# The order in which an instruction's semaphore waits are listed, for exponentials, turns, products and value products

## The chip, the cores and the metric

The kernel runs on one core of one Trainium2 chip. The metric is the device time in microseconds (us) of one execution, as the median of several runs. Besides the timed runs there is one execution taken by the hardware profiler; all durations below come from that one.

## What is computed

A small tower over 16 sequences of 512 tokens with 64 channels, in float32: token features, attention with 8 heads over one shared key and value, and a mixture of six experts of which two are taken per token. Cut to what matters here:

```python
h = tok(x, hour, month, day)                       # sines, two layers, layer norm, residual
n = layernorm(h)
q = einsum('bsc,oc->bso', n, Wq)                   # 8 heads of 64
k = einsum('bsc,oc->bos', n, Wk); v = n @ Wv       # one key and one value for all heads
attn = softmax(q k / sqrt(8))
h = h + (attn v, heads side by side) @ Wo
e = layernorm(h)
h = h + sum over the top two of six experts of weight * expert(e)
```

## The kernel before

The 16 sequences are worked in 8 pairs. The instructions of all five engines are written out by hand in one program; semaphores alone order the engines. A pair has 64 slots (`SLOTS`), and each step has the slot at which its engine issues it (the tables `A`, `P`, `F`, `Z`, `L` at the head of the file). In the slots of pair i the attention of pair i runs, beside the preparation of pair i+1 (`prep`) and the experts of pair i-1 (`ffn`).

- TensorE, `scores` (line 427; matmuls at 438): every second slot it writes two banks of scores of 128 x 512. `queries` (443, 450) makes the folded queries, `pv` (454, 470) multiplies the exponentials with the output weights scaled by one over the softmax sum, in two parts of 16 matmuls, for 64 groups of heads in all. `value_products` (553, 560) multiplies the turned result with the values. `turn_halves` (480), `values` (491), `tokens` (507, 518, 533), the router (602, 613) and the experts (627, 638, 662) fill the rest.
- VectorE: `maxima` (865, 868) takes minus the row maximum of each 128 x 512 scores and tells `maxed`; `recip_sums` (871, 874) inverts the sums and tells `rzd`; `turn` (876, 880) transposes the result of `pv` out of its bank and tells `mtd`.
- ScalarE: `exps` (736, 742) takes the exponential of a score bank into one of three kept buffers `p` and tells `expd`, 512 times; `queries_out` (748), `values_out` (758) and expert activations (796) copy other banks out.
- GpSimd (POOL): `over_sums` (289, 295) scales the output weights by the inverse sums and tells `wozd`.

All products land in four double banks (`s_bank`), which a planner (`ring_places`) hands out in the order of the program. Before a bank is written, `free` (387) waits for the step that read it last: `expd`, `mtd`, `gsb`, `e1_sb` and so on. The helper `wait` (280) skips waits for values of zero or less; its `wait_ge` is line 284. `pvd` tells that a `pv` is done, `fin_ps` that the value products of a pair are, `v_sb` that values were copied, `hatt_sb`, `y_ps`, `y_pool` belong to the experts' side.

An instruction can have several waits: the calls of `wait_ge` that stand between it and the instruction before it. The change touches nothing but their order.

Of the kernel before, what the change touches and what calls it, by code (L numbers as in the profile page):

```python
# [17 lines left out]
HH = HP // 2  # L18
# [26 lines left out]
KEPT = 3  # L45
# [136 lines left out]
def tower(nc, ids, consts, out):  # L182
# [4 lines left out]
    with ctx:  # L187
# [11 lines left out]
        def k(name):  # L199
            return cst[:, LAYOUT[name][0]:LAYOUT[name][1]]  # L200
# [48 lines left out]
        def bank(*what):  # L249
            return ring[place[what][0]]  # L250
# [29 lines left out]
        def wait(eng, s, value):  # L280

            if value <= 0:
                return
            eng.wait_ge(s, value)
# [95 lines left out]
        def _(pe):  # L380
            def half(r):
                return slice(64 * r, 64 * r + 64)

            def quarter(r):
                return slice(32 * r, 32 * r + 32)
# [68 lines left out]
            def pv(i, a, part):  # L454

                kept = (HH * i + a) % KEPT
                if part == 0:
                    free("PV", i, a)  # L460
                else:
                    pe.wait_ge(pv_half, HH * i + a + 1)
                for mm in range(4):
                    if not part and mm % 2 == 0:
                        pe.wait_ge(wozd, 2 * (HH * i + a) + mm // 2 + 1)
                    for r in range(2):
                        hh = (r + part) % 2
                        keys = p[half(r), 8 * kept + 2 * mm + hh, :].rearrange("q (n h o) -> q h n o", n=8, h=2)
                        for q in range(2):
                            last = pe.matmul(bank("PV", i, a)[half(q), 512 * hh:512 * hh + 256], woz[half(r), kept, 2 * mm + hh, :],  # L470
                                             keys[:, q, :, :], start=(part == 0 and mm == 0), stop=(part == 1 and mm == 3),
                                             skip_group_check=True)
                last.then_inc(pvd if part else pv_half, 1)
# [79 lines left out]
            def value_products(i, par, *heads):  # L553


                for n in range(8):
                    for g4 in range(4):
                        q, s2 = g4 // 2, g4 % 2
                        for b2, first, end in heads:
                            last = pe.matmul(  # L560
                                bank("FIN", i, s2)[half(b2), 512 * q + 32 * first:512 * q + 32 * end],
                                v[quarter(g4), par, b2, n, :], m[quarter(g4), b2, first:end, n, :],
                                start=(n == 0), stop=(n == 7), skip_group_check=True)
                return last

            def fin_part(n):

                i, par = PAIRS - 1, (PAIRS - 1) % 2
                if n == 0:
                    pe.wait_ge(v_sb, 2 * i + 2)  # L570
                pe.wait_ge(mtd, HH * i + HH - 2 + n)
                if n == 0:
                    free("FIN", i, 0)
                    free("FIN", i, 1)
                value_products(i, par, *(((0, 0, 8), (1, 0, 4)), ((1, 4, 6),), ((1, 6, 8),))[n]).then_inc(fin_parts, 1)

            def ffn(i, par, slot, f=F):

                if f is not L and slot == f["FIN"]:
                    pe.wait_ge(v_sb, 2 * i + 2)  # L580
                    pe.wait_ge(mtd, HH * i + HH)
                    free("FIN", i, 0)
                    free("FIN", i, 1)
                    value_products(i, par, (0, 0, HEADS), (1, 0, HEADS)).then_inc(fin_ps, 1)
                for n in (1, 2):
                    if f is L and slot == f["FIN" + str(n)]:
                        fin_part(n)
                if slot == f["T"]:
                    if f is L:
                        pe.wait_ge(ln_dve[2], LN_DVE * i + 1)  # L590
                        free("XT", i)
                        warm(WARM_T, bank("XT", i))
                    pe.wait_ge(ln_step[2], LN_STEP[2] * i + 3)
                    free("XT", i)
                    last = turn_halves(bank("XT", i), lambda t, rows, c: x2[rows, t, c, :], 4)
                    last.then_inc(x2t_ps, 1)
                if slot == f["R"]:
                    pe.wait_ge(xt_sb, i + 1)
                    free("R", i)
                    for c in range(2):  # L600
                        for r in range(2):
                            last = pe.matmul(bank("R", i)[half(c), 512 * r:512 * r + 256], k("rw1")[half(r), half(r)],  # L602
                                             xt[half(r), 256 * c:256 * c + 256], start=True, stop=True)
                    last.then_inc(rh_ps, 1)
                if slot == f["L"]:
                    pe.wait_ge(rh_sb, i + 1)
                    free("L", i)
                    for r in range(2):
                        for t in range(2):
                            for c in range(2):  # L610
                                for q in range(2):
                                    at_bank, first = 512 * c + NE * (2 * r + t), 256 * r + 128 * t + 64 * q
                                    last = pe.matmul(bank("L", i)[half(q), at_bank:at_bank + NE],
                                                     rh[half(c), first:first + 64],
                                                     k("rw2")[half(c), NE * c:NE * c + NE], start=True, stop=True,
                                                     skip_group_check=True)
                    last.then_inc(l_ps, 1)
                for e in range(EP):
                    if slot == f["E1"][e]:
                        if e == 0:  # L620
                            pe.wait_ge(xt_sb, i + 1)
                        free("E1", i, e)
                        double = bank("E1", i, e)
                        for r in range(2):
                            for q in range(2):
                                first = e * 128 + 64 * q
                                last = pe.matmul(double[half(q), 512 * r:512 * r + 512],  # L627
                                                 k("e1")[half(r), first:first + 64], xt[half(r), :],
                                                 start=True, stop=True)
                        last.then_inc(e1_ps, 1)  # L630
                    if slot == f["E2"][e]:
                        pe.wait_ge(e1_sb, EP * i + e + 1)
                        free("E2", i, e)
                        double = bank("E2", i, e)
                        for r in range(2):
                            for c in range(2):
                                first = e * 128 + 64 * r
                                last = pe.matmul(double[half(c), 512 * r:512 * r + 512],  # L638
                                                 k("e2")[half(r), first:first + 64],
                                                 e1t[half(r), e, 512 * c:512 * c + 512], start=True, stop=True)  # L640
                        last.then_inc(e2_ps, 1)
# [93 lines left out]
        def _(act):  # L735
            def exps(i, c):
                a, r = c // 8, c % 2
                act.wait_ge(maxed, SLOTS * i + c + 1)

                wait(act, pvd, HH * i + a - KEPT + 1)  # L740
                kept = (HH * i + a) % KEPT
                nc.scalar.activation(p[:, 8 * kept + c % 8, :], bank("S", i, c - r)[:, 512 * r:512 * r + 512], ACT.Exp,  # L742
                                     bias=nmax[:, c % 16:c % 16 + 1],
                                     accum_out=z[:, kept, c % 8:c % 8 + 1]).then_inc(expd, 1)
# [119 lines left out]
        def _(dve):  # L864
# [9 lines left out]
                nc.vector.reciprocal(rz[:, kept, :], z[:, kept, :]).then_inc(rzd, 1)  # L874

            def turn(i, a):
                dve.wait_ge(pvd, HH * i + a + 1)
                wait(dve, fin_ps, i)
                b2, n = a // 4, 2 * (a % 4)
                nc.vector.transpose(m[:, b2, n:n + 2, :, :].rearrange("q h n o -> q h (n o)"),  # L880
                                    bank("PV", i, a)[:, :].rearrange("q (h x) -> q h x", h=2)[:, :, 0:256]).then_inc(mtd, 1)
# [476 lines left out]
```

## Time and profile before

| | |
|---|---|
| median of 3 runs | 669.76 us (667.29 to 671.34) |
| profiled execution | 672.91 us |
| its span | 671.1 us |
| granted TensorE clock, mean | 0.983 |
| TensorE busy | 644.7 us, 96% |
| VectorE busy | 539.1 us, 80% |
| ScalarE busy | 476.0 us, 71% |
| GpSimd busy | 279.7 us, 42% |

The profiled execution is longer than its span by 1.8 us of start and end. PE is TensorE's matmuls, PEld its weight loads (issued by the same sequencer), DVE is VectorE, ACT is ScalarE, POOL is GpSimd. A matmul's end is modelled, so the start of the next one says more than an end. A "q" behind an engine's name means its sequencer. In the rows of the timeline the first column is the start in us from the span's start, the second the length in us from the first to the last of the merged instructions, "xN" their number, and a bracket the idle time of the engine before and what ended it.

### The profile page before, as it was taken

The page shows a single profiled execution, that of the slowest core. Times are in us where ns is not written, and L with a number is a line of the kernel's source. Part 1 is how long each engine was busy: PE and PEld are TensorE (multiplying, and loading weights), DVE is VectorE, ACT ScalarE, POOL GpSimd, SP SyncE. Part 2 cuts the span into 40 slices and gives each one's busy share as a digit, 9 for nine tenths or more (in the row PEclk, how much of TensorE's full clock was granted, in tenths as well). Part 3 has the DMA queues.
Part 4 walks back from the last instruction along what each step waited for, and adds up shares of the span by engine and source line. Part 5 has one row for each costly group of instructions (what it writes and reads, how often), then busy time and mean ns, then how long its engine had stood idle before and what let it go on. Part 6 is the DMA issues. An engine that isn't in the chain of part 4 may idle for free.

```text
span 671.1 us, 26756 instructions
## 1 busy us (share of the span) xinstructions
PE 644.7 (96%) x11632; PEld 360.9 (54%) x11632; DVE 539.1 (80%) x1068; ACT 476.0 (71%) x1193; POOL 279.7 (42%) x354
## 2 busy tenths in 40 slices
PE   7699999999999999999999999999999999999974
PEld 6345555555555466555655465555655555555653
DVE  4588678988788887989788887989889897977555
ACT  2388885887668866887668867697758875888331
POOL 1134112704763175622945156630947037311372
PEclk9799999999999999999999999999999999999978
DMA  4000000000000000000000000000000000000001
GB/s 173 1 2 2 2 2 3 2 2 2 19 4 2 2 3 19 3 2 2 4 19 2 2 3 20 2 2 3 3 19 2 2 3 19 2 2 2 4 2 32
DMA packets 9428, 6.66 MB, mean 10 GB/s; under 512 B 8672, under 2 KB 8672, under 8 KB 9184
## 3 DMA queue, kind: packets, MB, share of 16 engines
q1 hardware_dynamic: 9312, 4.97, 2.6%
q8 instruction: 91, 1.49, 1.0%
q14 instruction: 25, 0.20, 0.1%
HBM read 2.87 MB, written 2.10 MB: 7 GB/s over the span
## 4 chain that ended last, share of the span: by engine, by line
PE 90%; DVE 5%; ACT 2%; issue 1%; POOL 1%; DMA 1%; ACTq 0%; SPq 0%; DVEq 0%; POOLq 0%
PE s_bank L470 33%; PE s_bank L438 32%; PE s_bank L560 5%; PE s_bank L450 4%; PE s_bank L662 3%; PE s_bank L627 3%; PE s_bank L638 3%; PE s_bank L480 2%; ACT p L742 1%; PE s_bank L491 1%; PE s_bank L533 1%; PE s_bank L507 1%; PE s_bank L602 1%; PE s_bank L518 1%; POOL st L1177 1%
## 5 line engine op out<-in xcount | busy, mean ns | idle before, releaser
L742 ACT ACTIVATE p<-s_bank,nmax 128x512 f32<-128x512 f32 x512 | 347.3, 690 | 122.2 <-DVE nmax L868 121.7
L868 DVE TENSOR_REDUCE nmax<-s_bank 128x1 f32<-128x512 f32 x512 | 323.3, 681 | 36.2 <-PE s_bank L438 35.7
L438 PE MATMUL s_bank<-kf,g 64*64 64x512 f32 x2048 | 255.6, 597 | 1.1 <-DVE g L949 0.8
L470 PE MATMUL s_bank<-p,woz 64*64 64x256 f32 x4096 | 245.6, 378 | 1.8 <-ACT g L748 1.4
L470 PEld LDWEIGHTS s_bank<-p,woz 64*64 64x64 f32 x4096 | 153.6, 133 | 116.5 <-issue 37.6
L295 POOL TENSOR_TENSOR woz<-cst,rz 128x256 f32<-128x256 f32 x126 | 77.3, 634 | 246.9 <-DVE rz L874 246.9
L438 PEld LDWEIGHTS s_bank<-kf,g 64*64 64x64 f32 x2048 | 73.2, 134 | 91.2 <-issue 47.9
L742 ACT ACTIVATION_READ_ACCUMULATOR p<-s_bank,nmax 128x1 f32 x512 | 105.4, 206 | 0.0
L880 DVE STREAM_TRANSPOSE m<-s_bank 128x512 f32<-128x512 f32 x64 | 45.7, 714 | 24.5 <-PE s_bank L470 24.5
L1177 POOL TENSOR_TENSOR st<-st,power 128x8 f32<-128x8 f32 x24 | 39.5, 1644 | 37.7 <-DVE st L895 37.7
L304 POOL TENSOR_TENSOR y<-y,gt 128x768 f32<-128x768 f32 x28 | 41.3, 1475 | 17.6 <-DVE y L1094 17.6
L662 PEld LDWEIGHTS s_bank<-cst,e2t 64*64 64x64 f32 x1536 | 30.1, 141 | 11.8 <-issue 8.5
L450 PE MATMUL s_bank<-kf,qk 64*64 64x512 f32 x256 | 34.2, 605 | 0.9 <-DVE kf L945 0.9
L312 POOL TENSOR_TENSOR ys<-y 128x384 f32<-128x384 f32 x30 | 30.3, 1010 | 11.4 <-DVE y L1105 9.2
L748 ACT COPY g<-s_bank 128x1024 f32<-128x1024 f32 x31 | 31.1, 1004 | 4.4 <-PE s_bank L450 4.4
L1094 DVE TENSOR_TENSOR y<-s_bank,cst 128x768 f32<-128x768 f32 x28 | 26.7, 953 | 8.9 <-PE s_bank L662 6.8
L560 PE MATMUL s_bank<-m,v 32*64 32x256 f32 (+2 forms) x1152 | 32.1, 355 | 1.0 <-issue 1.0
L753 ACT ACTIVATE sq<-xc 128x512 f32<-128x512 f32 x24 | 15.0, 625 | 24.8 <-DVE xc L904 18.4
L662 PE MATMUL s_bank<-cst,e2t 64*64 64x64 f32 x1536 | 30.1, 225 | 1.2 <-ACT e2t L801 1.1
L560 PEld LDWEIGHTS s_bank<-m,v 32*64 32x64 f32 x1152 | 25.5, 131 | 10.4 <-issue 7.6
L796 ACT ACTIVATE e1t<-s_bank,cst 128x1024 f32<-128x1024 f32 x24 | 26.6, 1113 | 2.0 <-PE s_bank L627 0.5
L1079 DVE TENSOR_SCALAR e2t<-s_bank,cst 128x512 f32<-128x512 f32 x36 | 25.3, 744 | 0.7
(118 smaller groups left out, 504.4 us busy)
## 6 DMA issues: line engine op xcount, KB each, us to landing
tower_out<-o SPq DMA_DIRECT2D x16, 128.0 KB, 2.6
cst<-consts SPq DMA_DIRECT2D x1, 1070.0 KB, 8.5
e2t<-ids SPq DMA_DIRECT2D x1, 768.0 KB, 5.8
cst<-consts SPq DMA_DIRECT2D x1, 416.0 KB, 6.3
cst<-consts SPq DMA_DIRECT2D x1, 288.0 KB, 3.7
e2t<-ids SPq DMA_DIRECT2D x1, 256.0 KB, 3.5
cst<-consts SPq DMA_DIRECT2D x1, 3.0 KB, 1.8
```

The source lines that it names most:

```text
L295: ops.tensor_tensor(woz[:, kept, four, :].rearrange("q (m h) c -> q m h c", h=2), k("wo").rearrange("q (m c) -> q m c", m=4)[:, 2 * n:2 * ...
L304: ops.tensor_tensor(yt, yt, gt[:, 8, two, :].unsqueeze(3).to_broadcast([128, 2, NE, C]), ALU.mult).then_inc(y_pool, 1)
L438: last = pe.matmul(double[half(q), 512 * r:512 * r + 512], g[half(r), a // 2 % 2, a % 2, first:first + 64], kf[half(r), par, a // 4, :], s ...
L450: last = pe.matmul(double[half(q), 512 * r:512 * r + 512], qk[half(r), 2 * (quad % 2) + q, :], kf[half(r), par, quad // 2, :], start=True, ...
L470: last = pe.matmul(bank("PV", i, a)[half(q), 512 * hh:512 * hh + 256], woz[half(r), kept, 2 * mm + hh, :], keys[:, q, :, :], start=(part = ...
L560: last = pe.matmul(bank("FIN", i, s2)[half(b2), 512 * q + 32 * first:512 * q + 32 * end], v[quarter(g4), par, b2, n, :], m[quarter(g4), b2 ...
L662: last = pe.matmul(double[half(q), 512 * c + C * x:512 * c + C * x + C], e2t[half(c), x, first:first + 64], k("e3")[half(c), C * x:C * x + ...
L742: nc.scalar.activation(p[:, 8 * kept + c % 8, :], bank("S", i, c - r)[:, 512 * r:512 * r + 512], ACT.Exp, bias=nmax[:, c % 16:c % 16 + 1], ...
L748: nc.scalar.copy(g[:, quad % 2, :, :].rearrange("q n s -> q (n s)"), bank("Q", i, quad)[:, :]).then_inc(gsb, 1)
L868: nc.vector.tensor_reduce(nmax[:, c % 16:c % 16 + 1], bank("S", i, c - r)[:, 512 * r:512 * r + 512], AX.X, ALU.max, negate=True).then_inc( ...
L880: nc.vector.transpose(m[:, b2, n:n + 2, :, :].rearrange("q h n o -> q h (n o)"), bank("PV", i, a)[:, :].rearrange("q (h x) -> q h x", h=2) ...
L1177: nc.gpsimd.tensor_tensor(st[n][:, 4, :], st[n][:, 3, :], power[:, :], ALU.pow).then_inc(ln_step[n], 1)
```

## The change

It lists the same waits in another order, in four places. For an exponential the wait for the kept buffer (`pvd`) now comes before the wait for its maximum (`maxed`). For a turn the wait for the value products of an earlier pair (`fin_ps`) comes before the wait for its product (`pvd`). For the first product of a group the wait for the scaled weights (`wozd`) comes before the one for the bank (`free`). For the value products the wait for the turns (`mtd`) moves behind the two for the banks.

```diff
@@ pv, TensorE
                 kept = (HH * i + a) % KEPT
-                if part == 0:
-                    free("PV", i, a)
-                else:
+                if part:
                     pe.wait_ge(pv_half, HH * i + a + 1)
                 for mm in range(4):
                     if not part and mm % 2 == 0:
                         pe.wait_ge(wozd, 2 * (HH * i + a) + mm // 2 + 1)
+                    if not part and mm == 0:
+                        free("PV", i, a)
@@ ffn, TensorE
                     pe.wait_ge(v_sb, 2 * i + 2)
-                    pe.wait_ge(mtd, HH * i + HH)
                     free("FIN", i, 0)
                     free("FIN", i, 1)
+                    pe.wait_ge(mtd, HH * i + HH)
@@ exps, ScalarE
                 a, r = c // 8, c % 2
+                wait(act, pvd, HH * i + a - KEPT + 1)
                 act.wait_ge(maxed, SLOTS * i + c + 1)
-
-                wait(act, pvd, HH * i + a - KEPT + 1)
@@ turn, VectorE
+                wait(dve, fin_ps, i)
                 dve.wait_ge(pvd, HH * i + a + 1)
-                wait(dve, fin_ps, i)
```

## Rows read from the trace of the kernel before

**Rows 1.** The page, part 1: busy us, share of the span, instructions.
```profile
PE 644.7 (96%) x11632; PEld 360.9 (54%) x11632; DVE 539.1 (80%) x1068; ACT 476.0 (71%) x1193; POOL 279.7 (42%) x354
```

**Rows 2.** Busy time by engine in one middle pair (then PEclk, DMA share, GB/s).
```profile
325.00:402.00 77.00, 76.97 (x1428) 42.68 (x1424) 66.03 (x133) 58.10 (x147) 36.95 (x46) 1.00 0.03 6
```

**Rows 3.** Instructions of line 284: ns min/median/max, first and last start.
```profile
L284 ACTq EVENT_SEMAPHORE  x488: 17/17/17, 51.9 to 621.1; - x163
```

**Rows 4.** Instructions of line 465, the same columns.
```profile
L465 PEldq EVENT_SEMAPHORE  x64: 51/51/51, 39.3 to 626.9; - x64
```

**Rows 5.** Line 470: idle us of its engine and times, by what ended it.
```profile
  ACT p L742: 9.6, 23
  ACT g L748: 6.9, 6
  ACT e1t L796: 4.3, 6
```

**Rows 6.** Waits: who for whom, us in total, times, longest us.
```profile
ACT p L742 <- DVE nmax L868: 121.7, 141, 4.5
DVE m L880 <- PE s_bank L470: 24.5, 48, 2.5
```

**Rows 7.** Timeline, line 491 and the copy behind it, first pair and a middle pair.
```profile
66.96 2.19 PE L491 MATMUL s_bank<-kf,cst 64*64 64x512 f32 x16
68.06 1.07 ACT L758 COPY v<-s_bank 128x512 f32<-128x512 f32 x2
...
368.84 1.04 PE L491 MATMUL s_bank<-kf,cst 64*64 64x512 f32 x8
370.00 1.07 ACT L758 COPY v<-s_bank 128x512 f32<-128x512 f32 x2 [0.20 <-PE s_bank L491]
```

**Rows 8.** Timeline, two query copies and the products that they release.
```profile
355.80 1.00 ACT L748 COPY g<-s_bank 128x1024 f32<-128x1024 f32 x1
356.95 0.66 PE L602 MATMUL s_bank<-xt,cst 64*64 64x256 f32 x8
...
372.28 1.04 PE L438 MATMUL s_bank<-kf,g 64*64 64x512 f32 x8
374.75 1.00 ACT L748 COPY g<-s_bank 128x1024 f32<-128x1024 f32 x1
375.81 1.09 PE L438 MATMUL s_bank<-kf,g 64*64 64x512 f32 x8
```

**Rows 9.** Timeline, the group behind line 602.
```profile
357.53 1.50 PEld L470 LDWEIGHTS s_bank<-p,woz 64*64 64x64 f32 x32 [0.38 <-ACT p L742]
```

**Rows 10.** Timeline, from the next maxima to the next bound group.
```profile
361.42 1.28 DVE L868 TENSOR_REDUCE nmax<-s_bank 128x1 f32<-128x512 f32 x2
362.13 0.69 ACT L742 ACTIVATE p<-s_bank,nmax 128x512 f32<-128x512 f32 x1
362.76 0.50 PEld L613 LDWEIGHTS s_bank<-cst,rh 64*64 64x64 f32 x28 [0.21 <-issue]
363.37 0.21 PEld L438 LDWEIGHTS s_bank<-kf,g 64*64 64x64 f32 x8
365.37 0.69 ACT L742 ACTIVATE p<-s_bank,nmax 128x512 f32<-128x512 f32 x1
366.20 0.85 PEld L470 LDWEIGHTS s_bank<-p,woz 64*64 64x64 f32 x20
```

**Rows 11.** Timeline, from scores to the group behind an expert activation.
```profile
381.89 1.90 PE L438 MATMUL s_bank<-kf,g 64*64 64x512 f32 x16
383.69 0.69 ACT L742 ACTIVATE p<-s_bank,nmax 128x512 f32<-128x512 f32 x1 [0.44 <-DVE nmax L868]
386.19 1.50 PEld L470 LDWEIGHTS s_bank<-p,woz 64*64 64x64 f32 x32 [0.71 <-ACT e1t L796]
```

**Rows 12.** Timeline, an earlier query copy and the scores behind it.
```profile
335.83 1.01 ACT L748 COPY g<-s_bank 128x1024 f32<-128x1024 f32 x1 [0.73 <-PE s_bank L450]
336.89 0.21 PEld L438 LDWEIGHTS s_bank<-kf,g 64*64 64x64 f32 x8 [0.69 <-ACT g L748]
```

## The prediction

> **What bounds the kernel now.** I read the busy shares first: TensorE is busy 96% of the span, VectorE 80%, ScalarE 71% [rows 1]. Then one pair in the middle of the kernel: in 77.00 us TensorE is busy 76.97 at the full granted clock, ScalarE 58.10, VectorE 66.03 [rows 2]. So TensorE sets the time, and ScalarE and VectorE have room; what they do later costs only where TensorE then stands. A pair takes 77.1 us (the same bank wait recurs at that distance), and six of the eight pairs run alike.
>
> The next question is what a second wait of an instruction looks like in the trace. Line 284 is inside the helper `wait`. On ScalarE it appears as 488 EVENT_SEMAPHORE instructions: these are the exponentials' waits on `pvd`, which only the first 24 of 512 lack [rows 3]. Their wait on `maxed`, listed first, has no instruction of its own. On TensorE, line 465 (`wozd`, listed second) has 64, one per head pair [rows 4]. So the wait that is listed first rides on the instruction, and each further one becomes an instruction of the sequencer ahead of it. The change therefore adds and removes nothing: for 488 exponentials, 64 products and 56 turns it swaps which wait rides and which stands alone. For the exponentials and turns the late one now stands alone: `maxed` ends an idle stretch of ScalarE 141 times, `pvd` one of VectorE 48 times [rows 6], while `pvd` for an exponential is of the group three before it, and `fin_ps` for a turn older still. For products it is the bank's release: ScalarE's exponentials, query copies and first expert layer end 23, 6 and 6 of line 470's waits, POOL (`wozd`) none of those listed [rows 5].
>
> **The price of a late wait that stands alone.** ScalarE: the copy at line 758 has one wait in the first pair and two later, with the late one (`v_ps`) second. From the first matmul of line 491 to the copy it is 68.06 - 66.96 = 1.10 us with one wait and 370.00 - 368.84 = 1.16 with two [rows 7]: 0.06 us. TensorE: the same query copy releases a product with two waits at line 602, where the late one stands alone, and one with a single wait at line 438. The copies end at 356.80 and 375.75, the products start at 356.95 and 375.81: 0.15 against 0.06 us, so 0.09 more [rows 8]. VectorE shows no such pair in the rows here; I take 0.06 to 0.09.
>
> Advanced Engine Details and Errata of the Trainium skill, section Network/Comms, gives 50 to 100 ns for a sequencer's reading of a semaphore; the 0.06 and 0.09 above lie in that. The same page, section Sequencer Loop, says that other engine instructions can be read and queued while a control instruction is executed; taken at its word the exponential would be queued already when its separate wait passes, and the change would cost nothing. Line 758's 1.16 against 1.10 speaks against that.
>
> **The exponentials.** Of 488, those that find ScalarE idle start 0.06 later: at most 141. The others in a burst queue behind a predecessor and move with it. If all 141 lay on the path it would be 8.5 us; if TensorE never waited for them, 0.
>
> **The turns.** 48 x 0.06 to 0.09 = 2.9 to 4.3 us of VectorE time, in an engine that has 11 us free per pair. Behind a turn stand the reciprocal of the sums and the next maxima. Those mostly wait themselves for an exponential or for scores, and none of the bound waits below runs back through a turn that waited. I count 0, with 0 and 4.3 as the ends.
>
> **The products.** If TensorE finds the bank free, both orders cost one sequencer instruction that passes early. The extra 0.09 falls only where the bank is what it waits for. I went through the first matmul of each of the 64 groups: 24 start within 0.06 us of the release, three in each middle pair (357.54, 366.20, 386.19) and six outside. So 24 x 0.09 = 2.2 us, if nothing is taken back. `wozd`, which now rides, is never closer than 0.39 us before its product: no gain from it.
>
> **The value products** (six full ones with a `fin` group, and the last pair's are untouched): the three separate waits stay separate and only trade places. 0.
>
> **What reaches TensorE, in one middle pair** (325 to 402). Each bound wait is followed back to the matmul that set its chain off, and gets 0.06 for each idle-ending exponential on the way and 0.09 if it is a line-470 group:
> - 336.91, scores behind a query copy that ends at 336.84 [rows 12]: 0.07 us after the release, so next to bound; its chain grows 0.06, and 0.05 of it shows.
> - 356.95, router product behind the query copy: +0.06. Then 357.54 [rows 9], behind the next exponential of that burst: 0.06 + 0.09 = 0.15. But at 363.38 TensorE stands anyway for a turn: the loads of line 613 end at 363.26 and the next load starts at 363.37 [rows 10]. Going by starts that stall is 0.1 to 0.2 us. That turn's chain goes back over POOL and VectorE for 17 us with no waiting exponential in it, so it stays, and the 0.15 is covered there. 0.
> - 366.20: from the same VectorE chain over the maximum at 361.42, exponential 362.13, the reciprocal, more maxima, and exponential 365.37 [rows 10]: two exponentials and the bank, 0.06 + 0.06 + 0.09 = 0.21.
> - 375.81, scores behind a query copy [rows 8]: its chain starts at TensorE's scores at 372.28, so it comes on top: 0.06.
> - 386.19, behind an expert activation, from scores at 381.89 over exponential 383.69 [rows 11]: 0.06 + 0.09 = 0.15 on top.
>
> Sum: 0.05 + 0 + 0.21 + 0.06 + 0.15 = 0.47 us per middle pair, 2.8 us in six. The first pair has five bound line-470 groups; stalls for other reasons between them (0.05, 0.13, 0.25 us) take part back, and its first 24 exponentials don't change: 0.4. The last pair has one: 0.15. The tail after the last value products waits for none of the changed instructions. Total 3.4 us, so the span goes from 671.1 to 674.5 and the profiled execution from 672.91 to 676.3. That execution was 3.15 us above the median of 669.76; the median should move by the same 3.4, to 673.2.
>
> **The rivals.**
> 1. *Nothing shows.* Either the sequencer hides the wait, or later stalls take the delays back as at 363.38. For it: TensorE stands only about 1 us per pair in all, ScalarE is idle 19 of 77 us, and most exponentials' banks are released 0.2 to 2 us early. Against it: the stalls are set by loops that start at TensorE itself, so a longer loop can't be absorbed. Time: 0 to 1 us more, 670.3.
> 2. *More waits become bound.* After a separate wait that blocks, TensorE's queue starts empty; groups after a bound one already take 0.91 us instead of 0.86. If each of 24 costs another 0.05, and the turns' 4.3 us on VectorE reach TensorE by half, it is 3.4 + 1.2 + 2.2 = 6.8 us: 676.5.
> 3. *Faster.* If `wozd` and not the bank were what a product waits for, letting it ride would save 0.09 a group. It decides where POOL's scaled weights come later than the bank by more than the rest. Its lead is smallest at 0.39 us and its median is 1.7, so it needs a shift four times that of any chain above. At most 64 x 0.09 = 5.8 us, were all bound; with half of them, 667.
> 4. *The order makes no difference in the program*, because the builder sorts waits. Lines 284 and 465 show it doesn't for these. Included in the first.
>
> **How the numbers follow.** Forecast (2 to 5 us slower) 0.60, nothing shows 0.22, more 0.13, faster 0.05. The range holds the forecast, most of the second and the error of a median: 670.0 to 677.5. A half per cent, about what can be told from no change here, is 3.35 us, so the forecast lies right on that bound: a little over half of its 0.60 is above. Slower by over 0.5%: 0.36 + 0.13 = 0.49; within: 0.24 + 0.21 = 0.45, rounded to 0.46; faster 0.05.
>
> **What would show each step.** In the profile after: EVENT_SEMAPHORE with the line of the wait on `maxed` on ScalarE 488 times, and none for the `wozd` of a group's first product; the copies' and exponentials' idle-ending starts 0.08 rather than 0.02 us behind the maximum; line 470's bound groups 0.15 instead of 0.06 us behind the release; a middle pair of 77.5 to 77.7 us. Wrong would be: a pair still at 77.1 (absorbed), or pairs that grow by more than 0.8 with new bound groups.

## The result, and the profile after

| | before | after |
|---|---|---|
| median | 670.01 us (7 runs, 667.29 to 672.03) | 674.61 us (7 runs, 672.74 to 675.06) |
| ratio of the medians | | 1.0057 [1.0033, 1.0082] |
| profiled execution, its span | 672.91, 671.1 us | 674.95, 673.2 us |
| granted TensorE clock, mean | 0.983 | 0.985 |
| a pair in the middle, from scores to scores | 77.13 to 77.19 us | 77.53 to 77.76 us |

The kernel became 0.6% slower, by 4.6 us of the median; I had forecast 3.4. The page shows that no engine has more to do [rows 1]:

```profile
PE 645.5 (96%) x11632; PEld 389.5 (58%) x11632; DVE 537.9 (80%) x1068; ACT 476.2 (71%) x1193; POOL 280.0 (42%) x354
```

The counts are those of before, and TensorE's, VectorE's and ScalarE's busy time moved by under 1.3 us. One middle pair by engine, the counterpart of [rows 2] (length, busy us of PE, PEld, DVE, ACT and POOL with counts, granted clock, DMA share, GB/s):

```profile
326.25:403.79 77.54, 77.29 (x1428) 45.94 (x1424) 65.93 (x131) 58.12 (x147) 36.87 (x47) 1.00 0.03 6
```

The same 1428 matmuls at the same clock take 77.54 us. The weight loads (PEld) are busy longer in both views, 389.5 instead of 360.9 us in the whole, without a load more. That comes with the products' order: it is 393.4 us in e2_products and 388.9 in e6_after_first_only below, which have this order, and 361.2 in e1_exps, which has not. It doesn't follow the time, since e6_after_first_only has pairs 0.1 us shorter than the kernel after. The weight loads run beside the matmuls, and the starts of the matmuls decide.

The instructions of the line that waits for `maxed` (739 after the change), the counterpart of [rows 3], and who waits for whom (us in total, times, longest), the counterpart of [rows 6]:

```profile
L739 ACTq EVENT_SEMAPHORE  x488: 17/17/17, 53.2 to 625.0; - x163
...
ACT p L741 <- DVE nmax L867: 125.7, 140, 4.5
...
DVE m L879 <- PE s_bank L470: 28.3, 49, 2.4
```

So the program does what the change says: the late wait is now the separate instruction, 488 times, and line 465 (`wozd`) has none left. Perfetto Trace Analysis of the Trainium skill, section Identifying Dependency Chains, says that additional wait conditions may sit in EventSemaphore instructions ahead of the instruction; the trace agrees, with 488 of them, and adds which one they hold: all but the first listed. ScalarE waits 4.0 us longer for maxima in 140 waits, and VectorE 3.8 us longer for products in 49.

Line 470's idle time by what ended it, the counterpart of [rows 5]:

```profile
  issue: 54.9, 162
...
  POOL woz L295: 3.0, 9
  ACT g L747: 1.5, 1
  ACT p L741: 1.5, 7
```

This view must be read with care after the change. ScalarE ended 35 of these waits before and ends 8 now, and "issue" stands first with 162. The waits didn't go away: once the bank's release is a separate instruction, the view no longer ties it to the matmul. The time of the semaphore's update and the start of the matmul still stand in the trace, and by these 25 groups are bound by their bank instead of 24. The 9 waits put down to POOL are no waits for the scaled weights either: over all 64 groups `wozd` is never less than 0.38 us ahead of its product (0.39 before).

The starts in the middle pair that the prediction went through, the timeline of after (start us, busy us, engine, line, operation; an x8 or x32 in one row is a group):

```profile
337.11 1.94 PE L438 MATMUL s_bank<-kf,g 64*64 64x512 f32 x16
...
357.09 1.00 ACT L747 COPY g<-s_bank 128x1024 f32<-128x1024 f32 x1
358.23 0.66 PE L602 MATMUL s_bank<-xt,cst 64*64 64x256 f32 x8
358.91 1.96 PE L470 MATMUL s_bank<-p,woz 64*64 64x256 f32 x32
...
364.60 1.95 PE L438 MATMUL s_bank<-kf,g 64*64 64x512 f32 x16
367.64 1.73 PE L470 MATMUL s_bank<-p,woz 64*64 64x256 f32 x26 [0.16 <-ACT p L741]
...
376.25 1.00 ACT L747 COPY g<-s_bank 128x1024 f32<-128x1024 f32 x1
377.31 1.09 PE L438 MATMUL s_bank<-kf,g 64*64 64x512 f32 x8
...
386.58 1.11 ACT L795 ACTIVATE e1t<-s_bank,cst 128x1024 f32<-128x1024 f32 x1
387.84 1.53 PE L470 MATMUL s_bank<-p,woz 64*64 64x256 f32 x24
```

Set against [rows 8 to 11], the distance from the router product to the product behind it (358.23 to 358.91, before 356.95 to 357.54) grew from 0.59 to 0.68 us, and that from the copy to the router product (357.09 to 358.23) stayed at 1.14 to 1.15.

### The profile page after: what moved, and what is told of

Same layout as the page of the kernel before. It is cut to its first block, busy times and chain, and to the rows that moved or that the text cites. A ratio compares the mean times of both kernels' runs of the same rounds, so it can differ in the third digit from the quotient of the medians.

```text
span 673.2 us, 26756 instructions
## 1 busy us (share of the span) xinstructions
PE 645.5 (96%) x11632; PEld 389.5 (58%) x11632; DVE 537.9 (80%) x1068; ACT 476.2 (71%) x1193; POOL 280.0 (42%) x354
## 4 chain that ended last, share of the span: by engine, by line
PE 79%; DVE 9%; ACT 8%; issue 2%; POOL 1%; DMA 1%; SPq 0%; ACTq 0%; DVEq 0%; POOLq 0%
PE s_bank L470 30%; PE s_bank L438 27%; ACT p L741 7%; PE s_bank L560 5%; PE s_bank L627 3%; PE s_bank L450 3%; PE s_bank L662 3%; DVE nmax L867 3%; PE s_bank L638 3%; PE s_bank L491 1%; PE s_bank L533 1%; DVE st L884 1%; DVE h L966 1%; PE s_bank L507 1%; PE s_bank L480 1%
## 5 line engine op out<-in xcount | busy, mean ns | idle before, releaser
L470 PE MATMUL s_bank<-p,woz 64*64 64x256 f32 x4096 | 248.9, 380 | 3.4 <-ACT g L747 1.5
L470 PEld LDWEIGHTS s_bank<-p,woz 64*64 64x64 f32 x4096 | 173.1, 134 | 102.0 <-issue 54.9
L438 PEld LDWEIGHTS s_bank<-kf,g 64*64 64x64 f32 x2048 | 79.0, 134 | 83.5 <-issue 43.3
L627 PE MATMUL s_bank<-xt,cst 64*64 64x512 f32 x192 | 26.3, 619 | 0.0
```

Source lines behind the costliest of these rows:

```text
L438: last = pe.matmul(double[half(q), 512 * r:512 * r + 512], g[half(r), a // 2 % 2, a % 2, first:first + 64], kf[half(r), par, a // 4, :], s ...
L627: last = pe.matmul(double[half(q), 512 * r:512 * r + 512], k("e1")[half(r), first:first + 64], xt[half(r), :], start=True, stop=True)
```

## The experiments

Every kernel below computes the full result; none leaves work out. One ruler serves for all: TensorE's starts in the sixth pair, in which neither of the two odd delays of the last section lies. The timeline of TensorE, cut to seven instants (the narrow cuts also cut the counts at the end of a row), first before, then after:

```profile
401.95 0.61 PE L438 MATMUL s_bank<-kf,g 64*64 64x512 f32 x3
434.08 0.44 PE L602 MATMUL s_bank<-xt,cst 64*64 64x256 f32 x3
434.67 0.44 PE L470 MATMUL s_bank<-p,woz 64*64 64x256 f32 x3
440.52 0.66 PE L438 MATMUL s_bank<-kf,g 64*64 64x512 f32 x4
443.34 0.44 PE L470 MATMUL s_bank<-p,woz 64*64 64x256 f32 x3
463.33 0.44 PE L470 MATMUL s_bank<-p,woz 64*64 64x256 f32 x3
479.10 0.61 PE L438 MATMUL s_bank<-kf,g 64*64 64x512 f32 x4
```

```profile
403.57 0.59 PE L438 MATMUL s_bank<-kf,g 64*64 64x512 f32 x1
435.77 0.44 PE L602 MATMUL s_bank<-xt,cst 64*64 64x256 f32 x3
436.45 0.44 PE L470 MATMUL s_bank<-p,woz 64*64 64x256 f32 x3
442.14 0.65 PE L438 MATMUL s_bank<-kf,g 64*64 64x512 f32 x3
445.18 0.45 PE L470 MATMUL s_bank<-p,woz 64*64 64x256 f32 x4 [0.16 <-ACT p L741]
465.37 0.44 PE L470 MATMUL s_bank<-p,woz 64*64 64x256 f32 x3
481.11 0.59 PE L438 MATMUL s_bank<-kf,g 64*64 64x512 f32 x1
```

These are the counterparts of the points at 356.95, 357.54, 363.38, 366.20 and 386.19 in the prediction, 77.14 us later. The table gives the distances between them, from the same view of each kernel (us):

| kernel | scores to router product | to third group | to scores behind the turn | to fourth group | to sixth group | to next scores | pair |
|---|---|---|---|---|---|---|---|
| before | 32.13 | 0.59 | 5.85 | 2.82 | 19.99 | 15.77 | 77.15 |
| after | 32.20 | 0.68 | 5.69 | 3.04 | 20.19 | 15.74 | 77.54 |
| e1_exps | 32.24 | 0.59 | 5.78 | 2.94 | 20.12 | 15.76 | 77.43 |
| e2_products | 32.14 | 0.68 | 5.75 | 2.92 | 20.07 | 15.74 | 77.30 |
| e3_turns_values | 32.13 | 0.58 | 5.85 | 2.82 | 20.00 | 15.76 | 77.14 |
| e4_group2 | 32.13 | 0.68 | 5.76 | 2.82 | 19.99 | 15.77 | 77.15 |
| e5_groups35 | 32.14 | 0.59 | 5.84 | 2.92 | 20.07 | 15.74 | 77.30 |
| e6_after_first_only | 32.21 | 0.68 | 5.69 | 2.91 | 20.20 | 15.73 | 77.42 |
| e7_late_first | 32.04 | 0.68 | 5.84 | 2.82 | 20.00 | 15.76 | 77.14 |
| e8_before_first_only | 32.14 | 0.59 | 5.84 | 2.83 | 19.99 | 15.76 | 77.15 |
| e9_exps_two_separate | 32.35 | 0.58 | 5.71 | 3.10 | 20.27 | 15.82 | 77.83 |

The theory: a late wait that stands alone starts its instruction later by a fixed price, and the price reaches the end only where TensorE waits at the end of that chain. The rivals were that the sequencer hides it, that more waits become bound, and that the turns or the value products have a share.

### One part alone: e1_exps, e2_products, e3_turns_values

Only the exponentials have their waits in the new order:

```diff
+                wait(act, pvd, HH * i + a - KEPT + 1)
                 act.wait_ge(maxed, SLOTS * i + c + 1)
-
-                wait(act, pvd, HH * i + a - KEPT + 1)
```

> The kernel before with only the exponentials' two waits swapped. Theory (loops): each exponential that ends an idle stretch of ScalarE starts 0.05 to 0.06 us later, and that costs only where TensorE waits for the chain behind it: in a middle pair nothing at the router product (covered at the turn that TensorE waits for next), 0.11 at the group at 366, 0.05 at the scores at 376 and 0.05 at the group at 386. 0.21 us per pair, 1.3 in six, with the outer pairs 1.6 us, 0.24%. Rival (every swapped wait costs its sequencer time, 488 of them): 0.05 x 488 = 24 us of ScalarE time, at least several us more. Rival (only the product groups cost): no change.

Measured: 671.39 us, a ratio of 1.0032 [1.0017, 1.0046]. Of the six pairs from the second to the seventh, four are 0.24 to 0.30 us longer, two of these (the sixth and the seventh) by a further start that has become bound, of scores (in the sixth pair those at 409.18, 0.05 us later than their place; in the table it is a part of the 32.24); the third and the fifth are 0.49 and 0.46 longer (last section). A burst's maxima and its first exponential, in the timelines of before, of this kernel and of e9_exps_two_separate, at the same place of the pair:

```profile
450.49 1.29 DVE L868 TENSOR_REDUCE nmax<-s_bank 128x1 f32<-128x512 f32 x2 [0.70 <-PE s_bank L438]
451.22 0.69 ACT L742 ACTIVATE p<-s_bank,nmax 128x512 f32<-128x512 f32 x1 [0.44 <-DVE nmax L868]
```

```profile
452.23 1.29 DVE L867 TENSOR_REDUCE nmax<-s_bank 128x1 f32<-128x512 f32 x2 [0.70 <-PE s_bank L438]
453.01 0.69 ACT L741 ACTIVATE p<-s_bank,nmax 128x512 f32<-128x512 f32 x1 [0.49 <-DVE nmax L867]
```

```profile
451.96 1.29 DVE L871 TENSOR_REDUCE nmax<-s_bank 128x1 f32<-128x512 f32 x2 [0.70 <-PE s_bank L438]
452.83 0.69 ACT L745 ACTIVATE p<-s_bank,nmax 128x512 f32<-128x512 f32 x1 [0.57 <-DVE nmax L871]
```

From the first maximum to the exponential it is 0.73, 0.78 and 0.87 us. Read from the updates of `maxed`, an exponential that ends an idle stretch starts 24 ns behind it before and 83 ns here: 0.059 us, the 0.06 of the prediction.

Only the products have the new order (the exponentials, turns and value products the old one):

```diff
-                if part == 0:
+                swapped = True
+                if part:
+                    pe.wait_ge(pv_half, HH * i + a + 1)
+                elif not swapped:
                     free("PV", i, a)
-                else:
-                    pe.wait_ge(pv_half, HH * i + a + 1)
...
+                    if not part and mm == 0 and swapped:
+                        free("PV", i, a)
```

> The kernel before with only the first product's waits swapped. Theory (loops): 24 bound groups start 0.09 us later behind the release; in a middle pair the one behind the router product is covered by the wait for the turn, the ones at 366 and 386 show: 0.18 us per pair, 1.1 in six, and some 0.4 in the outer pairs: 1.5 us, 0.22%. Rival (TensorE's sequencer stands at the bank in all 64 groups and its queue starts empty): 64 x 0.09 = 5.8 us or more. Rival (only the exponentials cost): no change.

Measured: 671.31 us, 1.0026 [1.0006, 1.0046]; five pairs 0.15 to 0.17 us longer, the fifth 0.55 (last section). In the table three distances grow, by 0.09, 0.10 and 0.08, and the one to the scores behind the turn shrinks by 0.10. A bound group starts 45 ns behind the update of its bank before and 136 ns here.

Only the turns and the value products have the new order:

```diff
@@ value products, TensorE
-                    pe.wait_ge(mtd, HH * i + HH)
                     free("FIN", i, 0)
                     free("FIN", i, 1)
+                    pe.wait_ge(mtd, HH * i + HH)
@@ turn, VectorE
+                wait(dve, fin_ps, i)
                 dve.wait_ge(pvd, HH * i + a + 1)
-                wait(dve, fin_ps, i)
```

> The kernel before with the waits of the turns and of the value products swapped, and nothing else. Theory (loops): turns that end an idle stretch of VectorE start 0.07 us later, 2.9 us in sum over 42 of them, but no chain that TensorE waits for goes through one: middle pairs keep their 77.13 us, 0 us. Rival (VectorE's time counts): up to 3 us more, with the scores' maxima later by 0.07 behind each turn.

Measured: 669.19 us, 1.0000 [0.9978, 1.0022], and a pair of 77.14 us. The turns do start later: VectorE waits 27.5 us for line 470 in 48 waits instead of 24.5, 0.06 us more for each, and nothing comes of it.

What follows: the exponentials and the products make the loss and hardly touch each other. The steps of a pair, read at the starts of TensorE, are 0.24 and 0.155 us alone and 0.40 together; the ratios are 1.0032, 1.0026 and 1.0057. The sequencer doesn't hide the wait.

### Which groups carry the products' share: e4_group2, e5_groups35

The products' new order for the third group alone, in the six middle pairs, and then for the fourth and the sixth:

```diff
+                swapped = a == 2 and 1 <= i < PAIRS - 1         # e4_group2
+                swapped = a in (3, 5) and 1 <= i < PAIRS - 1    # e5_groups35
+                if part:
                     pe.wait_ge(pv_half, HH * i + a + 1)
+                elif not swapped:
+                    free("PV", i, a)
...
+                    if not part and mm == 0 and swapped:
+                        free("PV", i, a)
```

> The kernel before, with the first product's waits swapped in one group per middle pair only: the third, that behind the router product (357.54), which is bound. Theory (covered): its start moves 0.09 us behind the release, and the wait for a turn six us later takes all of it back; a middle pair keeps its 77.13 us. Rival (every bound wait costs): 0.09 us more per middle pair, 0.5 in six.

> The kernel before, with the first product's waits swapped in two groups per middle pair: the fourth (366.20) and the sixth (386.19), both bound with nothing behind them that TensorE waits for on another chain. Theory: both 0.09 us stay, a middle pair takes 77.13 + 0.18 = 77.31 us. Rival (taken back later, as with the third group): 77.13.

Each has one time only (667.33 and 672.98 us, beside 670.51 for the kernel before), so here the pairs decide. Three starts of e4_group2, counterparts of 434.08, 434.67 and 440.52:

```profile
431.43 0.44 PE L605 MATMUL s_bank<-xt,cst 64*64 64x256 f32 x3
432.11 0.44 PE L473 MATMUL s_bank<-p,woz 64*64 64x256 f32 x3
437.87 0.66 PE L438 MATMUL s_bank<-kf,g 64*64 64x512 f32 x4
```

The group starts 0.68 instead of 0.59 us behind the router product, and the scores behind the turn 6.44 us behind it, as before. The delay is real and is taken back whole six microseconds later, where TensorE waits for a turn that does not depend on it. e5_groups35 keeps the pair's first distances and has the whole share of the products: 77.30 us, as e2_products. So of the three bound groups per pair two cost and one is covered.

### Which exponentials matter, and whether the separate instruction itself costs: e6_after_first_only, e8_before_first_only

All eight exponentials of a group wait for the same value of `pvd`; the first is enough. Here the other seven don't list it, with the order of after and of before:

```diff
+                if c % 8 == 0:
+                    wait(act, pvd, HH * i + a - KEPT + 1)
                 act.wait_ge(maxed, SLOTS * i + c + 1)           # e6: order of after
```

```diff
                 act.wait_ge(maxed, SLOTS * i + c + 1)           # e8: order of before
-                wait(act, pvd, HH * i + a - KEPT + 1)
+                if c % 8 == 0:
+                    wait(act, pvd, HH * i + a - KEPT + 1)
```

> The changed kernel, but only the first exponential of each group of eight waits for the kept buffer; the other seven have the maximum's wait alone, so it rides on them. Theory (loops): the exponentials in the chain to the group at 366 are the 8th of one group and the 2nd of the next, so that chain gets its 0.11 us back; the chains to 376 and to 386 begin with the first of a group and keep their 0.05. A middle pair then takes 0.40 - 0.11 = 0.29 us more than before, and the whole 0.7 us less than the changed kernel. Rival (the number of separate waits counts): 427 fewer of them, so clearly faster than the kernel before as well.

> The kernel before with the wait for the kept buffer on the first exponential of each group of eight alone, so 427 sequencer instructions of ScalarE fewer, all of which pass early. Theory: middle pairs keep 77.13 us, 0 us. Rival (each sequencer instruction costs, also where it passes at once): 427 x 0.02 to 0.06 = 8 to 25 us of ScalarE's time less, and some of it in the whole.

Measured: e6_after_first_only 671.99 us, 1.0040 [1.0020, 1.0060]; its six pairs are 0.28 to 0.30 us longer than before instead of 0.40. Its last scores before the fourth group, and that group:

```profile
439.18 0.66 PE L438 MATMUL s_bank<-kf,g 64*64 64x512 f32 x4
442.09 0.44 PE L470 MATMUL s_bank<-p,woz 64*64 64x256 f32 x3
```

2.91 us, against 2.82 before and 3.04 after: the 0.12 of the two exponentials on that chain, which aren't the first of their group, is gone, and the 0.09 of the bank is left. This shows the sum of that step, 0.06 + 0.06 + 0.09, term by term.

e8_before_first_only: 669.07 us, 1.0002 [0.9979, 1.0025]. 427 separate instructions fewer (26329 instead of 26756 in all) change no pair but the fifth (last section), to speak of. A separate wait that is long fulfilled costs nothing here. Only a late one does.

### Is a second one charged again: e9_exps_two_separate

Before every exponential but the first 24 stand four waits; `pvd` rides, and the other three fill two separate instructions, the late one in the first of them. The two added waits are for loads that are long done:

```diff
+                wait(act, pvd, HH * i + a - KEPT + 1)
+                if HH * i + a >= KEPT:
+                    act.wait_ge(load_qk, 16)
                 act.wait_ge(maxed, SLOTS * i + c + 1)
+                if HH * i + a >= KEPT:
+                    act.wait_ge(load_rest, 16)
-                wait(act, pvd, HH * i + a - KEPT + 1)
```

> The kernel before with the exponentials' waits swapped, as in the run with the exponentials alone, and with two more waits that are always long fulfilled (the loads of the constants). The maximum's wait then stands alone in a first sequencer instruction and the two idle ones in a second behind it. Theory (the sequencer must still work through everything between the late wait and the instruction): exponentials that end an idle stretch start some 0.11 to 0.14 us behind the maximum instead of 0.08, and a middle pair takes twice the 0.24 us of the single swap, 0.45 to 0.5 us more than before. Rival (only where the late wait stands counts, not what follows it): 0.08 us and 0.24 us per pair as before.

Measured: 675.08 us, 1.0074 [1.0051, 1.0097]. The wait for maxima of the whole kernel (same columns as above), and the two separate instructions:

```profile
ACT p L745 <- DVE nmax L871: 128.7, 140, 4.5
...
L741 ACTq EVENT_SEMAPHORE  x488: 17/17/17, 51.1 to 625.4; - x163
...
L743 ACTq EVENT_SEMAPHORE  x488: 38/38/38, 51.2 to 625.5; - x163
```

The exponentials start 161 ns behind the maximum, after 24 and 83: a second separate instruction behind the late wait costs 0.078 us more. But the pair grew by 0.67 to 0.71 us in four of six (the second by 0.90 and the fifth by 1.09, last section), where I expected 0.45 to 0.5. With 0.137 us for an exponential, e1's steps scale to 0.24 x 0.137 / 0.059 = 0.56. The rest are scores that weren't bound before, with the group behind them: the group at 409.18 is 0.08 later than its place in the pair, and the one at 475.19 is 0.06 later. So here the rival "more waits become bound" has begun, at somewhat over twice the price that the change has; the 0.05 in two pairs of e1_exps is its first trace. In the middle pairs of the change itself it isn't needed.

### The other direction: e7_late_first

If a late wait should ride, two places of before could gain: the router product, whose bank release stands second behind `xt_sb`, and the value copies, whose `v_ps` stands behind `fin_ps`:

```diff
@@ router product, TensorE: the bank's release first
-                    pe.wait_ge(xt_sb, i + 1)
...
+                    pe.wait_ge(xt_sb, i + 1)
@@ values_out, ScalarE: v_ps first
-                wait(act, fin_ps, kk - 1)
...
+                wait(act, fin_ps, kk - 1)
```

> The kernel before with the late wait listed first in two more places: the bank (a query copy) for the router product at 357, and the value product's end for the value copies. Theory: the router product starts 0.06 instead of 0.15 us behind the copy, but the group behind it waits for the next exponential and at 363 TensorE waits for a turn, so middle pairs keep 77.13 us: no gain. Rival (each bound wait counts by itself): 0.09 us per pair less, 0.5 us in six.

Measured: 670.37 us, 1.0003 [0.9982, 1.0023]. The router product and the group behind it:

```profile
433.81 0.45 PE L602 MATMUL s_bank<-xt,cst 64*64 64x256 f32 x4
434.49 0.45 PE L470 MATMUL s_bank<-p,woz 64*64 64x256 f32 x4
```

The router product comes 0.09 us sooner (32.04 instead of 32.13 us into the pair) and the next group waits 0.09 longer, since its exponential is as late as before. In the second to the seventh pair the first value copy starts 24 instead of 78 ns behind its product, and no start of TensorE moves with it. The price has the same size in both directions, and the path doesn't get shorter by it. No kernel of this study is faster than the one before by more than can be told.

## Why the prediction held, and where its steps were off

**The order of the waits.** Right: the first listed rides and the rest stand alone, for 488 exponentials and 64 products.

**The prices.** 0.06 us for an exponential, measured 0.059. 0.09 for a product, measured 0.091. 0.06 to 0.09 for a turn, measured 0.070. These came from two pairs of like chains in the trace of before [rows 7, 8], and that was enough. Advanced Engine Details and Errata of the Trainium skill, section Sequencer Loop, would have had the next engine instruction queued while the separate wait is executed; the measured 59, 70 and 91 ns on three engines speak against that reading for a wait that blocks. Where the wait passes early, e8_before_first_only shows no cost, as that reading would have it.

**336.91, scores behind a query copy, +0.05.** Wrong, it is 0. The copy there, after the change:

```profile
336.89 1.01 ACT L747 COPY g<-s_bank 128x1024 f32<-128x1024 f32 x1 [0.67 <-PE s_bank L450]
```

The copy comes 1.06 us later than before (335.83 to 336.89). So do the scores behind it: they are the second half of the row that begins at 337.11 (before at 336.05), and their weight loads start at 337.95 (before 336.89). The pair itself began 1.05 later (324.76 to 325.81). The copy waits directly for a matmul of line 450, as the bracket in [rows 12] already said. There is no exponential on that chain, and I charged one.

**356.95 and 357.54, +0.15, covered.** Right, with e4_group2 for the product's 0.09 and e1_exps for the exponential's 0.06 (its distance to the scores behind the turn is 5.78 instead of 5.85).

**366.20, +0.21.** Right: 3.04 - 2.82 = 0.22, taken apart by e1, e2 and e6 into 0.12 and 0.09.

**375.81, +0.06, and 386.19, +0.15.** Right: together 20.19 - 19.99 = 0.20.

**The sum of a pair.** Mis-sized: 0.40 instead of 0.47 us; the pairs grew by 0.39 to 0.42 in four of six. Nearly all of the difference is the first item (0.05). The other two grew by 0.57 and 0.61. Six pairs together: 2.78 us, forecast 2.8. That these agree is partly luck, and so is the agreement of the whole: about 0.37 of it are the two odd places below and would not have been there by my steps.

**First and last pair.** The first pair's first group starts 0.09 us later behind its release, in a stretch that ran at another granted clock. From the second part of that group on, the pair grows by 0.14 - 0.16 + 0.21 - 0.09 + 0.15 + 0.14 = 0.39 us, where stalls took back part, as expected in kind; forecast 0.4 in all. The last pair grows by 0.15 for the group that I named, by 0.05 for another that started 0.18 us behind its release before and is the 25th bound one, and by 0.05 at the products of line 613, which I had not listed: 0.25, forecast 0.15.

**The turns.** VectorE waits 3.8 us more in all for 49 of them, and e3_turns_values shows 0 in the time: the lower of the two bounds, which I took.

**The whole.** From the second part of the first group to the value products of the last pair, the timelines of TensorE, before and then after:

```profile
43.50 1.04 PE L470 MATMUL s_bank<-p,woz 64*64 64x256 f32 x16
...
623.61 0.68 PE L560 MATMUL s_bank<-m,v 32*64 32x256 f32 x21
```

```profile
42.75 1.72 PE L470 MATMUL s_bank<-p,woz 64*64 64x256 f32 x28
...
626.32 0.47 PE L560 MATMUL s_bank<-m,v 32*64 32x256 f32 x9
```

580.11 us became 583.57, so 3.46 longer: 0.39 in the first pair, 2.78 in the six, 0.29 in the last (0.04 more than the steps above, which leave out that single starts sit up to 0.03 us off their place in the products' order). The forecast was 3.4. The two profiled spans differ by 2.1 only. The kernel after takes 0.75 us less up to this stretch and 0.61 less behind it; it ran by another granted clock there (next section; behind it 0.97 from 634 to 647 us, and 0.87 before from 632 to 645). The medians differ by 4.6 us. With the interval of the ratio, 2.2 to 5.5 us, the 3.46 is inside; what makes the medians differ by a further 1.1 isn't shown by any trace. It may be nothing but the spread of single runs: those of before differ by some 5 us, and among 21 of them 668.34 us came with a mean granted clock of 0.993 and 672.61 us with 0.984.

## What to carry to other kernels

Where an instruction has several waits, find out which one the builder lets ride (here the first listed) and list the one that comes last in time first: a late wait that stood alone cost 0.06 to 0.09 us each time, an early one nothing. It matters only where the bound engine stands at the end of that chain and no later stall takes it back, so follow each bound wait to the matmul that set it off before summing, and take every link from the rows: the one link that I assumed (336.91) was the one that was wrong. Once a wait stands alone, views of idle time by releaser may call it "issue"; compare starts, not the releasers.

## What the runs showed of the hardware

**A late separate wait.** From the update of the semaphore to the start: ScalarE 24 ns riding, 83 ns alone, 161 ns alone with another separate instruction behind it; VectorE 24 and 94 ns; TensorE 45 and 136 ns. The latter two of ScalarE don't follow the durations of the separate instructions (17 and 38 ns).

**The clock at both ends differs between executions.** TensorE's granted clock in the same stretch, before and then after (the clock is the third number from the end of each row):

```profile
27.00:36.00 9.00, 8.20 (x48) 2.09 (x44) 4.47 (x7) 6.03 (x12) 1.62 (x1) 0.58 0.01 2
```

```profile
27.00:36.00 9.00, 7.54 (x68) 1.92 (x64) 5.72 (x11) 8.00 (x19) 1.62 (x1) 1.00 0.01 2
```

Before was at a mean of 0.58 there, so mostly at the lower of the two levels (1.2 GHz), and after at the full 2.4; after had its stretch of lower clock later, at a mean of 0.76 from 36 to 43 us. In the eleven profiled executions of this study the second pair starts anywhere between 90.39 (e3_turns_values) and 93.50 us (e1_exps). A profiled span can thus be off by 3 us at its start alone, which is nearly the whole effect that was asked for. Between, at the full clock, the same pair of different kernels agrees to 0.01 us where nothing of it was touched (77.14 or 77.15 five times in the table, before included); the ruler rests on that.

**Two places with a delay of their own.** In the third pair of after and e1_exps two exponentials in a row are 0.2 us further apart than elsewhere. ScalarE's timeline of after, and of before at the same place:

```profile
230.32 0.19 ACT L741 ACTIVATION_READ_ACCUMULATOR p<-s_bank,nmax 128x1 f32 x1
230.61 0.69 ACT L741 ACTIVATE p<-s_bank,nmax 128x512 f32<-128x512 f32 x1
```

```profile
229.94 0.19 ACT L742 ACTIVATION_READ_ACCUMULATOR p<-s_bank,nmax 128x1 f32 x1
230.03 0.68 ACT L742 ACTIVATE p<-s_bank,nmax 128x512 f32<-128x512 f32 x1
```

0.29 against 0.09 us from the one start to the next. No instruction is recorded between the two rows, but the place is a special one. It is the 576th of ScalarE's recorded instructions, and a packet of 8192 bytes with instructions starts on DMA queue 14 at 231.25, 0.64 us behind it. One more exponential is as late in both kernels (363 ns behind its maximum), 896 = 7 x 128 records further on, again with such a packet 0.64 or 0.65 us behind it. In e9_exps_two_separate two of them start 440 instead of 161 ns behind their maximum, at 150.81 and 614.46 us, and these are 1664 = 13 x 128 records apart; the first makes its second pair longer. No other exponential that found ScalarE idle is late like this in the three kernels. In before the same exponential starts 105 ns behind its maximum, with nothing lost. So this delay goes with one place in every 128 of ScalarE's records, with an instruction packet close behind, and shows only where an exponential at that place has a late separate wait.

The other delay is that of the value products in the fifth pair. The program's 64 products are 128 matmuls in the trace. From their first start to the start of the group behind them they take 3.63 or 3.64 us in every kernel in the six other pairs that have all of them in one piece. In the fifth pair a packet of 16384 bytes with instructions on DMA queue 8 lands meanwhile (that queue has 91 of them in before, one for some 258 of TensorE's recorded instructions), and the later it lands, the longer they take (us from their first weight load):

| kernel | packet starts | packet lands | the products take |
|---|---|---|---|
| e4_group2 | -0.54 | 0.39 | 3.64 |
| e3_turns_values | -0.34 | 0.59 | 3.64 |
| e7_late_first | 0.56 | 1.64 | 3.69 |
| before | 0.65 | 1.73 | 3.69 |
| e6_after_first_only | 0.78 | 1.74 | 3.72 |
| after | 0.90 | 1.86 | 3.86 |
| e1_exps | 0.93 | 1.98 | 3.86 |
| e2_products | 0.78 | 2.06 | 4.08 |
| e9_exps_two_separate | 0.87 | 2.07 | 4.08 |
| e5_groups35 | 1.32 | 2.25 | 4.26 |
| e8_before_first_only | 1.32 | 2.25 | 4.28 |

e8_before_first_only has the order of before and the longest delay, so the order isn't its cause. The table fits matmuls that wait for their own instructions, but that is read from the traces alone: no experiment was made on either delay, and what makes the packet start late in some kernels stays open. The two make up the uneven pairs above.
